# Reads of q and k issued by two engines, and a new order of steps on every engine

## The reference, cut to what matters

```python
# layer 0: graph attention with 20 neighbours, two directions d, 16 heads of 16
self_feat = concat(x, q_exp) @ W_self.T + b_self       # 256x512 by 512x256
for d in range(2):
    qh = self_feat @ Wq[d].T + bq[d]; kh = self_feat[:20] @ Wk[d].T + bk[d]
    aff = where(mask[d], qh . kh / 4, NEG) + label_bias[d]
    w = softmax(aff)                                   # 256 x 16 x 20
    output += (w @ self_feat[:20]) . Wout[d] + bout[d]
x1 = x + relu(output)
# layer 1: transformer block, 16 heads of 16, feed-forward width 1024
nx = rmsnorm(x1) * w_norm1 * (1 + scale) + shift       # scale, shift from cond
q, k, v = nx @ wq + bq, nx @ wk + bk, nx @ wv + bv     # q, k rotated by position
x2 = x1 + softmax(q k.T / 4) v @ wo + bo               # 256x256 scores for each head
nz = rmsnorm(x2) ...
out = x2 + (gelu(nz @ w_gate) * (nz @ w_up)) @ w_down
```

## Time and profile before

| | us |
|---|---|
| median of 3 runs | 570.43 (569.77 to 572.45) |
| the profiled execution | 569.02 |
| its span, first to last instruction | 567.4 |
| PE busy | 468.3 (83%) |
| VectorE busy | 325.0 (57%) |
| ScalarE busy | 237.7 (42%) |
| GpSimd busy | 231.2 (41%) |
| mean granted clock of TensorE | 0.943 |

### The profile page before, as it was taken

The page is one execution under the profiler, slowest core; times in us unless marked ns, Lnnn a source line. Parts: engine busy times, 40 slices in busy tenths (PEclk is TensorE's granted clock), DMA queues, the critical chain, the costliest instruction groups (busy, mean ns, idle before and its releaser), DMA issues. The chain is left out here.

```text
span 567.4 us, 9625 instructions
## 1 busy us (share of the span) xinstructions
PE 468.3 (83%) x3644; PEld 397.0 (70%) x3644; DVE 325.0 (57%) x597; ACT 237.7 (42%) x465; POOL 231.2 (41%) x203
## 2 busy tenths in 40 slices
PE   0387773878799979998999899989998898699567
PEld 0266462756599858985898589858986796498366
DVE  0835676585685667566856686667664753461111
ACT  3115221125444553555355545454555346227222
POOL 0735167228324822482348233823382253211022
PEclk9996695599999999999999999999999999889879
DMA  8812202502801080109010901090009003600000
GB/s 281 301 43 74 88 1 92 94 2 72 186 1 63 10 205 2 57 16 204 2 49 25 204 1 41 32 205 1 22 2 203 1 3 120 86 1 3 20 0 20
DMA packets 33276, 40.22 MB, mean 71 GB/s; under 512 B 3152, under 2 KB 28240, under 8 KB 32976
## 3 DMA queue, kind: packets, MB, share of 16 engines
q1 hardware_dynamic: 33232, 39.61, 27.1%
HBM read 28.85 MB, written 10.49 MB: 69 GB/s over the span
## 5 line engine op out<-in xcount | busy, mean ns | idle before, releaser
L1081 PE MATMUL ps<-splz,wh 128*128 128x256 f32 x512 | 98.9, 288 | 3.0 <-POOL splz L377 3.0
L942 DVE TENSOR_REDUCE nm<-ps 128x2 f32<-128x512 f32 x128 | 84.5, 688 | 17.8 <-PE ps L1277 16.7
L603 ACT ACTIVATE ya<-ps 128x512 f32<-128x512 f32 x128 | 72.0, 599 | 52.6 <-PE ps L1301 51.1
L377 POOL TENSOR_TENSOR hs<-g,hs 128x512 fp32r<-128x512 f32 x32 | 41.4, 1293 | 107.1 <-ACT hs L659 107.1
L1081 PEld LDWEIGHTS ps<-splz,wh 128*128 128x128 f32 x512 | 80.7, 194 | 5.5 <-issue 5.4
L1081 PE MATMUL ps<-splz,wl 128*128 128x256 f32 x256 | 72.9, 285 | 0.0
L1277 PE MATMUL ps<-kst,qst 96*128 96x256 f32 x256 | 52.8, 306 | 6.2 <-DVE nm L942 3.0
L1081 PE MATMUL ps<-wh,hs 128*128 128x256 f32 x256 | 55.8, 285 | 0.8 <-POOL hs L377 0.8
L1301 PE MATMUL ps<-qst,kst 100*128 100x256 f32 x256 | 53.5, 306 | 2.4 <-ACT ya L603 1.5
L649 ACT ACTIVATE g<-ps 128x512 f32<-128x512 f32 x32 | 19.2, 600 | 72.8 <-PE ps L1081 72.8
L1081 PEld LDWEIGHTS ps<-splz,wl 128*128 128x128 f32 x256 | 49.4, 193 | 0.0
(11 more groups left out here) (136 smaller groups left out, 970.7 us busy)
## 6 DMA issues: line engine op xcount, KB each, us to landing
qk_d<-ya SPq DMA_DIRECT2D x16, 512.0 KB, 2.8
qst<-qk_d SPq DMA_DIRECT2D x24, 256.0 KB, 5.1
kst<-qk_d SPq DMA_DIRECT2D x48, 128.0 KB, 5.9
adjD<-adj SPq DMA_DIRECT2D x8, 440.0 KB, 4.1
ya<-wall SPq DMA_DIRECT2D x12, 256.0 KB, 4.5
xT<-xt SPq DMA_DIRECT2D x8, 256.0 KB, 2.7
x_add<-x SPq DMA_DIRECT2D x8, 256.0 KB, 3.7
result<-xr SPq DMA_DIRECT2D x8, 256.0 KB, 3.1
```

Of the source, the lines that this page charges most:

```text
L377: pool.tensor_tensor(into, whole, high.bitcast(FP32), ALU.subtract).then_inc(signal.sem, 1)
L603: act.activation(ex[:, h % EXR], ps[:, h % 2].rearrange("p (c s) -> p c s", c=TC), ACT.Exp, scale=SCALE).then_inc(ex_ok.sem, 1)
L942: dve.tensor_reduce(nm[:, :, h], ps[:, h % 2].rearrange("p (c s) -> p c s", c=TC), AX.X, ALU.max, negate=True).then_inc(mx_ok.sem, 1)
L1081: ins = pe.matmul(dst, lhs(a, k), rhs(c, k), start=first_ and n == 0 and m == 0, stop=last_ and n == len(ks) - 1 and m == 2, **kw)
```

## The change

The function `stack` is split. SP issues the six reads of k in `kstack`; ACT issues the three reads of q in a new step `qstack`, with the same waits. Then the steps in the lists of all five engines stand in another order, and some are called with another `it`. What a step does is unchanged. The diff, cut; every list is reordered from its first line to its last:

```diff
-            def stack(b):
+            def kstack(b):
 ...
-                for part, at in ((0, 0), (0, 64), (1, 32)):
+                for part, at in ((0, 0), (0, 32), (1, 64)):
                     if part == 1:
                         sp.wait_ge(lo_out.sem, lo_out.at(b))
-                    sp.dma_start(qst[at:at + 32, :, :].bitcast(FP32), qk_d[part, 0:D].rearrange("(q r) s -> r q s", r=32)).then_inc(stack_in.sem, 16)
                     for e in range(2):
-                        at_k = {(0, 0): 0, (0, 64): 32, (1, 32): 64}[(part, at)] + DH * e
+                        at_k = at + DH * e
 ...
 # SP's list
-                step(stack, it - 1)
 ...
-                step(nrows, it - 1)
 ...
-                step(load_xt, it + 2)
-                step(load_adj, it + 2)
 ...
-                step(load_x_add, it + 1)
-                step(store_hi, it)
-                step(store_lo, it)
+                step(load_adj, it + 1)
+                step(load_x_add, it)
 ...
+                step(store_hi, it - 1)
+                step(load_xt, it + 2)
+                step(store_lo, it - 1)
+                step(kstack, it - 1)
+                step(nrows, it - 1)
                 step(store, it - 2)
 # ACT: the new step, and its place
+            def qstack(b):
+                if b:
+                    act.wait_ge(st_ps.sem, st_ps.at(b - 1))
+                else:
+                    act.wait_ge(zero_ok.sem, zero_ok.at(0))
+                act.wait_ge(hi_out.sem, hi_out.at(b))
+                for part, at in ((0, 0), (0, 64), (1, 32)):
+                    if part == 1:
+                        act.wait_ge(lo_out.sem, lo_out.at(b))
+                    act.dma_start(qst[at:at + 32, :, :].bitcast(FP32), qk_d[part, 0:D].rearrange("(q r) s -> r q s", r=32)).then_inc(stack_in.sem, 16)
 ...
                 step(pTa(1), it)
+                step(qstack, it - 1)
                 step(square2, it - 2)
 ...
-                step(aexp(0), it + 1)
-                step(xh, it + 1)
+                step(aexp(0), it)
+                step(xh, it + 2)
 # POOL's list, first and last lines
+                step(aprob(1), it)
+                step(qklow(1), it - 1)
                 step(x1bias, it - 1)
 ...
+                step(aadd(0), it + 1)
+                step(xl, it + 2)
+                step(hlow(3), it - 2)
+                step(asub(0), it + 1)
 ...
+                step(asub(1), it + 1)
                 step(aprob(0), it + 1)
                 step(qklow(0), it)
-                step(asub(1), it + 1)
-                step(qklow(1), it)
 # DVE's list, first and last lines
+                step(pTv(0), it)
+                step(qkadd(1), it - 1)
 ...
                 step(onorm(0), it - 2)
                 step(onorm(1), it - 2)
 ...
                 step(mx(5), it - 1)
+                step(xr_scaled, it)
 ...
                 step(qkadd(0), it)
-                step(qkadd(1), it)
-                step(result, it - 2)
                 step(asums(1), it + 1)
-                step(pTv(0), it + 1)
 # PE's list
-                step(st(12), it - 2)
+                step(qkT(0), it - 1)
                 step(st(13), it - 2)
                 step(pv(2), it - 2)
                 step(st(14), it - 2)
+                step(qkT(1), it - 1)
                 step(st(15), it - 2)
+                step(pTt(0), it)
                 step(pv(3), it - 2)
 ...
+                step(q0(1, 0), it + 1)
+                step(nxT, it)
                 step(down(0, 1), it - 2)
+                step(down(1, 1), it - 2)
                 step(affm(0), it + 1)
+                step(st(0), it - 1)
+                step(st(1), it - 1)
                 step(up(3, 1), it - 2)
+                step(up(3, 0), it - 2)
                 step(affm(1), it + 1)
 ...
                 step(qk(0), it)
-                step(qk(1), it)
 ...
                 step(st(6), it - 1)
-                step(qkT(0), it)
                 step(st(7), it - 1)
-                step(qkT(1), it)
+                step(qk(1), it)
+                step(down(2, 0), it - 2)
                 step(st(8), it - 1)
                 step(st(9), it - 1)
                 step(pv(1), it - 1)
-                step(pTt(0), it + 1)
                 step(st(10), it - 1)
+                step(down(3, 1), it - 2)
                 step(st(11), it - 1)
-                step(down(3, 1), it - 2)
+                step(down(3, 0), it - 2)
+                step(st(12), it - 1)
```

More of the change, by code:

```diff
@@ L313, in round_ @@
             def round_(it):
+                once(weights("qk", 1), it + 3)
+                once(weights("d", 0), it)
+                once(weights("o", 0), it + 1)
+                once(weights("q0", 0), it + 3)
+                once(weights("self", 0), it + 3)
+                once(weights("q0", 1), it + 2)
+                once(weights("u", 0), it)
+                once(weights("g", 1), it)
+                once(weights("v", 0), it + 2)
+                once(weights("g", 0), it + 3)
+                step(load_adj, it + 1)
@@ L314, in round_ @@
+                once(get_wkv, it + 1)
+                step(load_x_add, it)
+                once(weights("u", 2), it - 1)
+                once(weights("u", 3), it - 1)
+                once(weights("u", 1), it + 1)
+                once(weights("qk", 0), it + 2)
+                once(weights("g", 2), it + 2)
+                once(get_vec, it + 3)
+                once(weights("d", 1), it)
                 once(get_wb, it + 2)
                 once(weights("g", 3), it + 2)
-                step(stack, it - 1)
@@ L710, in round_ @@
                 step(hh(1), it - 2)
-                step(q0c(1), it + 1)
-                step(nrowc, it - 1)
-                step(gelu(3), it - 2)
+                step(nrowc, it - 1)
+                once(whigh("g", 2), it + 3)
+                step(q0c(0), it + 1)
+                once(whigh("u", 0), it)
+                step(gelu(3), it - 2)
+                step(q0c(1), it + 1)
+                once(whigh("q0", 1), it + 2)
+                step(nxc, it)
+                once(whigh("self", 0), it + 3)
@@ L1002, in round_ @@
             def round_(it):
+                step(pTv(0), it)
+                step(qkadd(1), it - 1)
+                once(ones(0), it + 1)
+                once(ones(1), it)
+                once(wlow("u", 0), it - 1)
                 step(onorm(0), it - 2)
+                once(rotated_bias, it + 3)
                 step(onorm(1), it - 2)
                 step(pTv(1), it)
+                once(zeros(0), it + 3)
                 step(al, it - 2)
@@ L1403, in round_ @@
                 step(aT, it - 2)
+                step(pTt(3), it)
+                step(wo(1), it - 2)
+                step(wo(0), it - 2)
+                step(y, it)
                 step(v(1), it - 1)
-                step(pTt(3), it)
-                step(wo(0), it - 2)
-                step(wo(1), it - 2)
-                step(y, it)
                 step(x1T, it)
@@ L1458, in round_ @@
                 step(affm(1), it + 1)
-                step(st(0), it - 1)
-                step(up(3, 0), it - 2)
-                step(st(1), it - 1)
                 step(down(1, 0), it - 2)
+                step(st(2), it - 1)
+                step(st(3), it - 1)
                 step(qk(0), it)
-                step(qk(1), it)
-                step(st(2), it - 1)
                 step(down(2, 1), it - 2)
-                once(cond_q, it + 2)
-                step(st(3), it - 1)
-                step(down(2, 0), it - 2)
```

206 lines of the change are left out of this document (85 added, 121 removed).

## The result

The changed kernel takes 611.43 us (median of 4 runs, 610.41 to 615.75), against 570.1 us of the kernel before beside it: 1.073 times the time, 95% interval 1.068 to 1.078. The forecast was 585, the range ended at 599. The sign was right; 41 us were lost where 15 were forecast.

A forecast was written before the change was run, and what follows sets the result against it. TensorE (PE) was taken to bound the kernel, q and k's trip through memory 1 to 3 us behind. Terms -2.5 + 2.3 + 12.5 + 3.7 - 1.0 = +15.0 on 569.02 gave 584.0, as median 585 us; range 566 to 599.

The forecast's parts named there:

- start, up to s(0) of batch 0: Run's start: first attention-score product of batch 0 comes 2.5 us earlier, bounds 4.7 earlier and 2 later.
- batch 0 to 1: Round without the feed-forward part: 47.75 us becomes 50.0, +2.3, bounds 0 and 4.
- batches 1 to 7: Five full rounds at 2.5 us longer each, +12.5, then batch 6 to 7, +3.7.
- behind the last s(0): Run's end: the last scores meet no q/k work and start sooner, 1 us gained.
- The clock falls in every round: Scores behind each stall: TensorE at half clock, 2 us a round lost, 595 us in all; chance 0.22.
- rival 1: TensorE's clock falls behind the stall in every round, 2 us a round, 595 us; chance 0.22.
- The reading term: q and k reads before the next s(0): 11.3 us, plus 0.8 charged for the second store ahead of them.
- Positions of stores: q and k's stores in a full round: issued at 44.7 and 47.1 us after s(0), 4.4 and 5.5 later than before.
- The late trip: q and k's later way through memory: next s(0) at 59.6 us, PE ready at 55.7 and standing 3.9.
- I count no hole in the transfers: Reads in a full round: ScalarE reaches its q reads near 49 us, while the four first k reads are queued.
- the second issuer: q reads issued by ScalarE: same 16 engines, only issue time saved, so the reading phase keeps its 11.3 us.
- Rival 2: Reads: two queues run beside each other and shorten the phase, at 6.9 us 555 in all; chance 0.13 of being faster.

The follow-up runs named there:

- e6: Changed kernel with 40 filler matrix products on TensorE in front of the wait for the nine reads, from batch 1 on: 602.19 us, ratio 1.058.
- e9: Kernel before with q and k's trip through memory moved late, pTt(0) and pTv(0) moved late with it: 607.39 us, ratio 1.067.
- e1: Kernel before with the three q reads issued by ScalarE behind pTa(1), everything else as before: 569.37 us, ratio 1.001.
- e2: Changed kernel with all nine reads issued by SyncE again, other steps in the changed order: 610.77 us, ratio 1.073.
- e8: Changed kernel with the load of the next xT (256 KB) moved behind the k reads: 613.67 us, ratio 1.080.
- e7: Changed kernel with qklow(1) in front of aprob(1) on GpSimd and qkadd(1) in front of pTv(0) on VectorE: 608.39 us, ratio 1.070.
- e11: Changed kernel with qklow(1) before aprob(1), qkadd(1) before pTv(0), and the xT load behind the k reads: 597.46 us, ratio 1.048.
- e12: Changed kernel with q and k's trip early, one read issuer, adj, x_add and xT loads behind the reads, and the trip's feeders moved to match: 591.13 us, ratio 1.037.
- e13: Changed kernel with qklow(1) and qkadd(1) earlier, xT load behind the k reads, and ten filler products before the reads' wait: 591.88 us, ratio 1.039.
- e14: Kernel before with 18 filler products on TensorE in front of the wait for batch 7's reads alone: 568.31 us, ratio 0.998.

## Why the prediction was wrong

The terms of the sum against the traces:

| term | forecast | measured | from |
|---|---|---|---|
| start, up to s(0) of batch 0 | -2.5 | +2.3 | 112.27 against 109.98 |
| batch 0 to 1 | +2.3 | +6.9 | 54.63 against 47.75 |
| batches 1 to 7 | +12.5 + 3.7 | +35.2 | 369.12 against 333.95 |
| behind the last s(0) | -1.0 | +2.2 | 77.9 against 75.7 |
| sum | +15.0 | +46.5 | |

Of the 35.2 us, 27.5 fall on the five full rounds (forecast 12.5) and 7.7 on the last (3.7). So about 15 of the 31.5 us that are missing lie in the full rounds, 8.6 in the two lighter ones and 8.0 at start and end.

- **The step that failed: "The clock falls in every round" was left a rival, at 0.22, and its 2 us a round stayed out of the sum.** Behind stalls of 3.75 to 5.50 us the clock fell each time, to 0.50 to 0.54. Its size was right (2.0 us a round, e6): 10 of the 15 us missing in the full rounds. The trace of before had the whole mechanism at batch 7; having forecast a stall of 3.9 us, more than batch 7's 2.37, I had no row of a stall as long as that which left the clock up. The condition was met by my own number, so it belonged in the forecast. The Trainium skill, "TensorE: Matmul & The Clock Gate", section "HAM oscillation — how this bites in real kernels", tells of a kernel in which every tile starts cold behind its DMA wait; the trace after agrees (0.50 behind batch 4's stall).
- How the clock reaches the next round, rival 1 did not say. A round that begins at 0.50 reaches pv(3) at 45.3 and the first store at 47.1 (45.7 to 47.1 over the five full rounds); in e6 the store is at 44.3 to 44.4. The store waits for work that runs behind the slow scores, so the time lost in the scores is not absorbed by the stall but delays the store and the next s(0). In e6 TensorE waits for the reads as long as before, only its fillers keep it busy meanwhile.
- **The reading term was mis-sized**, by about 1 us a round. I measured from the first read (11.3) and charged 0.8 for the store in front: 12.1 from the first k read to s(0), with 12.8 as the upper bound; it is 13.1 in the round of batch 3. From the second store to s(0) I had 12.5, and it is 13.5 with and without the clock's fall. In the trace of before the way from the second store to the last landing was 12.6 in the round of the earlier trace rows (313.56 to 326.2), but 11.6 to 14.7 over the eight batches, 13.1 on average, and 13.6 at batch 7, where it ended the wait. That average, taken from the store, would have carried over to within half a microsecond.
- Positions of stores: right in a full round at full clock, 44.4 and 47.0 in e6 for 44.7 and 47.1. In the lighter rounds the first store came later than forecast: at 38.7 after s(0) of batch 0 for 35.4, and at 41.8 after that of batch 6 for 38.2 (37.5 and 40.4 in e6). The late trip makes the stall, as forecast (e9).
- "I count no hole in the transfers" and the second issuer: right (e1, e2). Rival 2 is out.
- The xT load got no word. In the changed list it stands between the two stores. At their distance of 2.57 us it costs nothing (e8); it only spoils the obvious repair (e7, e11).
- Start: forecast 2.5 earlier, measured 2.3 later, with the first store at 97.0 instead of 93.1. Batch 0 to 1: a round that begins cold too. Behind the last s(0) 2.2 us were lost where I had a gain of 1. Start and end were not tried by themselves and stay open; e9 and e12 put them down to the new order more than to the late trip (-1.5 and +0.8 in e9, +5.1 and +4.2 in e12).

What isn't settled: e6 gives 9 of the 41 us to the clock by medians. Added to the old order, the late trip with its clock costs 38; taken out of the new order, it gives back 20 (e12). So the stall and the clock are shown as causes, but how the 41 us divide between the late trip and the rest of the new order is not.

## What to carry to other kernels

When a change makes the bounding engine wait for a transfer, look in the trace for what happened to its clock behind a wait as long as that, and put it into the sum, not among the rivals. Measure a chain of transfers from the last event that holds it up (here the second store), over all rounds of the trace and not in one alone. And a step is moved only with all that feeds it: three of these experiments moved a chain without one of its feeders and were 35 to 56 us slower than the versions in which its feeders, and some neighbours, were moved too.

## What the runs showed of the hardware

- The stall's length alone did not tell whether the clock falls: in e11 it stayed at 1.00 behind 2.75 us and was 0.64 behind 2.63 us, while filling 1.2 us of such stalls kept it at 1.00 behind the first scores of batches 1 to 5 (e13).
- The clock also fell without any long stall: in e14 it was 1.00 in 476 to 480 us, 0.59 in 480 to 484 and 0.50 in 484 to 490, and TensorE's longest single wait between 476 and 490 was 0.94 us; in the trace of before it was 1.00 from 476 to 489.
- One load of 256 KB between two stores 1.35 us apart lengthened the way from the first store to s(0) by 2.1 us (16.8 in e7 against 14.7 in e11, batch 4; 1.6 to 3.3 over batches 1 to 4); between stores 2.57 us apart, taking it away gained nothing (e8).
